# Two mixture-of-experts layers on one core: expert rows stored by halves and blended in place, first loads and the tile table moved ahead of the borders

## The chip, the cores and the metric

The kernel runs on one core of a Trainium2 chip. The metric is the device time of one launch in microseconds (us); the median of 3 runs before the change is 739.51 us (737.39 to 741.89). The engines are TensorE (PE, with its weight loads as PEld), VectorE (DVE), ScalarE (ACT), GpSimd (POOL) and SyncE (SP). SP and ACT issue plain DMAs, POOL issues indirect ones (scatters whose destination rows come from an index tile).

## The reference

32 sequences of 128 tokens with 128 channels (4096 tokens) pass through two layers.

- Layer 0: each sequence is scaled by a style vector made from its condition, projected, normalised by a factor, biased and clipped. Then a feed-forward stage: every token chooses the 2 best of 8 experts (`top_k` of `x @ Wg`), their weights are a softmax of the two logits, each expert computes `silu(x W1) * (x W2) @ W3` with 176 hidden channels, and a shared expert of 352 hidden channels is added.
- Layer 1: an adapter conditioned on the sequence (128 to 32 to 128, ReLU, residual); then layernorm, attention with 16 heads of 8 channels and a residual; then layernorm, again the 2 best of 8 experts, each `relu(h W1 + b1) @ W2 + b2` with 512 hidden channels, weighted and added to the stream. The output is `(32, 128, 128)` float32.

What matters for the change: each token ends as `x + w_a * expert_a(h) + w_b * expert_b(h)`, a sum of its stream row and two expert rows.

## The kernel before

`build` runs six blocks one after another: `layer0`, `experts0`, `pre_attention`, `attention`, `experts1`, `finish`. Each block gives every engine its own instruction list; a block ends with a barrier of all engines. SBUF holds the stream `m.X` (partition = token in the sequence, 32 sequences of 128 channels), and the arrays `m.V` (attention's values) and `m.X3` (the stream after the adapter) of the same shape.

**Routing.** Tokens go in 8 groups of 4 sequences. `choose_*` (DVE) finds the two best experts, `route_rank` (PE) counts places within an expert, `index_*` (DVE) gives each (token, choice) a row of the DRAM buffer `dispatch_rows`, and POOL scatters the rows there (`route_scatter`, L341, 8 indirect DMAs of 128 rows per group). Each row carries 128 channels, its destination row in `expert_rows` (slot `SLOT_ID`, copied from `m.ids` at L310) and its softmax weight. The destination row of (sequence s, token p, choice k) is `2 * (128 s + p) + k`, so the two rows of a token lie side by side; the choice is 0 for the better expert.

**The tile table.** Each expert's rows are cut into tiles of 256; there are always 39 tiles (`ETILES`), the most that can be needed, and those past the last real one hold padding rows. After the last group, `table_vector` (DVE, L397 to L420) computes for every tile its expert and its first row; its first instruction (L397) writes where each expert's rows end and raises `ended`, its last ones raise `tabled`. On `ended`, SP fills the rest of the last tile of experts 0 to 3 with padding (`table_fill`, L371) and ACT that of experts 4 to 7. SP then waits for all fills to land (`tails`); POOL waits for all scatters. Then comes the barrier.

**Experts.** In `experts0` and `experts1` SP reads for every tile two entries of the table (`value_load`) and issues two DMAs: 256 rows (`xs` at L859, `xt` at L1841, 130 KB) and the expert's weights (`w` at L861, 304 KB; `wb` at L1843, 578 KB). There are 8 load buffers (`EB`). PE turns the rows (L766), multiplies in three float32r products (L816) and projects down (L893, L1872); ACT and DVE split and evacuate; POOL scatters two times 128 rows per tile to `expert_rows` (L825). PE's order at the start is: turn tile 0, turn tile 1, up-products of tile 0, then for each n: turn n + 2, up n + 1, down n. In `experts1` the last step on a tile is DVE's `leave` (L1883), which adds the bias, and POOL's scatter follows.

**Finish.** SP fetches the two rows of each token in 8 groups of 512 KB (`fetch_rows`, L948) into 4 buffers, DVE adds the first row to `m.X` (L978) and the second to that (L981), and ACT stores each group of 256 KB (L987).

In `attention` DVE's list carries, beside the softmax work of sequence s, the routing of earlier groups cut into pieces between the maxima (L1570): `choose_hot` (L280, L281), `index_place` (L305 to L314).

## Time and profile before

| what | value |
|---|---|
| profiled execution, its own time | 738.1 us |
| its span, first to last instruction | 736.3 us |
| median of 3 runs | 739.51 us |
| PE busy, share of span | 588.9 us, 80% |
| DVE busy | 490.2 us, 67% |
| POOL busy | 448.7 us, 61% |
| ACT busy | 370.1 us, 50% |
| mean granted TensorE clock | 0.903 |

The span is from the first to the last instruction of the profiled execution; its own time is 1.8 us longer and takes in what lies around it. The engines' busy times are sums over stages with different limits, so no one of them is the time: the page's slices show PE at 9 tenths or more in the two expert stages and in attention, and well below that in the slices (18 us each) before either expert stage is under way and at the end.

### The profile page before, as it was taken

To read this page: it belongs to the slowest core of one execution; us is meant where nothing else is said; L and a number is where in the kernel's file an instruction comes from. 1 tells how busy PE (TensorE), PEld (TensorE's weight loads), DVE (VectorE), ACT (ScalarE), POOL (GpSimd) and SP (SyncE) were. 2 spreads that over 40 slices of the span, in tenths; PEclk is the share of its full clock that TensorE was granted. 3 is DMA by queue.
4 is the path that set the end of the run, shared out by engine and by line. 5 is a ranking of instruction groups with operands and counts; after the bars stand their busy time and mean duration, and the time that the engine had idled before them with its cause. 6 is when DMAs were issued, how large, how long until landed. Compare 5 with 4: busy or idle time off the path is not lost. (4 is left out here: it accounts for less than half of the span.)

```text
span 736.3 us, 17755 instructions
## 1 busy us (share of the span) xinstructions
PE 588.9 (80%) x5538; PEld 473.9 (64%) x5538; DVE 490.2 (67%) x1502; ACT 370.1 (50%) x798; POOL 448.7 (61%) x588
## 2 busy tenths in 40 slices
PE   4999935999992787737999999999920999999940
PEld 2566625989892555415766766676620999999940
DVE  3566434767671689755878878877652678878735
ACT  3444303655561344335777777777520556556520
POOL 2677741766677658274455887797763256666640
PEclk9999976999996599967999999999955899999985
DMA  7911146767773267715553444444117988888429
GB/s 223 244 57 52 55 94 163 213 198 207 201 212 103 71 187 220 222 68 104 102 119 85 132 108 132 105 125 123 44 40 162 314 258 246 260 242 248 138 66 314
DMA packets 97978, 115.24 MB, mean 157 GB/s; under 512 B 16144, under 2 KB 77616, under 8 KB 97776
## 3 DMA queue, kind: packets, MB, share of 16 engines
q1 hardware_dynamic: 82368, 92.36, 46.8%
q0 software_dynamic: 9088, 18.76, 7.8%
q10 hardware_dynamic: 6448, 3.20, 1.8%
q8 instruction: 38, 0.62, 0.4%
q14 instruction: 36, 0.29, 0.2%
HBM read 80.75 MB, written 33.53 MB: 155 GB/s over the span
## 5 line engine op out<-in xcount | busy, mean ns | idle before, releaser
L341 POOL DMA_INDIRECT dispatch_rows<-row,index x128 | 126.0, 984 | 56.9 <-issue 33.7
L825 POOL DMA_INDIRECT expert_rows<-fo,to x78 | 84.0, 1076 | 68.2 <-DVE fo L1883 54.8
L1570 DVE TENSOR_REDUCE mneg<-ps 128x4 f32<-128x512 f32 x128 | 86.6, 679 | 43.4 <-PE ps L1711 42.6
L825 POOL DMA_INDIRECT expert_rows<-eo,to x78 | 74.7, 958 | 52.6 <-ACT eo L918 30.2
L1661 ACT ACTIVATE prob<-ps 128x512 f32<-128x512 f32 x128 | 75.4, 589 | 54.2 <-PE ps L1723 53.5
L798 DVE CAST xh<-psT 128x256 fp32r<-128x256 f32 x78 | 33.1, 424 | 73.8 <-PE psT L766 73.6
L1872 PE MATMUL psO<-wb,fh 128*128 128x128 f32 x624 | 75.9, 275 | 0.0
L1711 PE MATMUL ps<-km,qp 96*128 96x512 f32 x128 | 63.2, 500 | 14.0 <-POOL km L1508 12.7
L1654 ACT ACTIVATE km<-kp,const 96x512 fp32r<-96x512 f32 x96 | 67.7, 712 | 11.0 <-PEq L1045 5.5
L816 PE MATMUL psA<-xh,wh 128*128 128x256 f32 (+1 forms) x234 | 73.1, 312 | 0.0
L1872 PEld LDWEIGHTS psO<-wb,fh 128*128 128x128 f32 x624 | 73.1, 192 | 0.0
L816 PE MATMUL psA<-xh,wl 128*128 128x256 f32 (+1 forms) x234 | 66.7, 285 | 0.0
L816 PE MATMUL psA<-xl,wh 128*128 128x256 f32 (+1 forms) x234 | 66.6, 285 | 0.0
L1508 POOL TENSOR_SCALAR km<-kp,const 96x512 fp32r<-96x512 f32 x32 | 54.4, 1701 | 14.4 <-POOLq L1045 13.0
L1721 PE MATMUL ps<-qm,kp 96*128 96x512 f32 x128 | 52.3, 409 | 3.0 <-DMA qm<-qk_parts 2.9
L1723 PE MATMUL ps<-mxT,selr 128*128 128x512 f32 x128 | 51.4, 402 | 0.0
L1918 ACT ACTIVATE fw<-psO,xt 128x128 f32<-128x128 f32 x78 | 24.4, 364 | 44.1 <-PE psO L1872 28.8
L1711 PEld LDWEIGHTS ps<-km,qp 96*128 96x128 f32 x128 | 25.5, 200 | 28.4 <-issue 21.4
L790 ACT ACTIVATE wh<-w 128x352 fp32r<-128x352 f32 x39 | 19.4, 497 | 47.3 <-DMA w<-in_W 44.8
L816 PEld LDWEIGHTS psA<-xl,wh 128*128 128x128 f32 (+1 forms) x234 | 42.7, 183 | 0.0
L816 PEld LDWEIGHTS psA<-xh,wh 128*128 128x128 f32 (+1 forms) x234 | 42.7, 182 | 0.0
L816 PEld LDWEIGHTS psA<-xh,wl 128*128 128x128 f32 (+1 forms) x234 | 42.5, 182 | 0.0
(193 smaller groups left out, 1505.2 us busy)
## 6 DMA issues: line engine op xcount, KB each, us to landing
wb<-in_W1b SPq DMA_DIRECT2D x39, 578.0 KB
w<-in_W SPq DMA_DIRECT2D x39, 304.0 KB
qk_parts<-qk SPq DMA_DIRECT2D x8, 1024.0 KB, 5.0
qp<-qk_parts SPq DMA_DIRECT2D x48, 128.0 KB, 2.8
kp<-qk_parts SPq DMA_DIRECT2D x48, 128.0 KB, 3.4
qm<-qk_parts SPq DMA_DIRECT2D x192, 32.0 KB
xs<-dispatch_rows SPq DMA_DIRECT2D x39, 130.0 KB
xt<-dispatch_rows SPq DMA_DIRECT2D x39, 130.0 KB
```

The lines of the kernel that those rows point to most:

```text
L341: pool.indirect_dma_start(out=m.xbuf, out_offset=bass.IndirectOffsetOnAxis(ap=r.index[b][:, c:c + 1], axis=0), in_=r.row[b][:, c // TOPK, ...
L798: v.tensor_copy(z.xh[q][:], z.psT[:, q, 0:SLOTS]).then_inc(z.x_high, 1)
L816: ins = z.m.nc.tensor.matmul(out, w[k][q][:, columns], x[k][q][:], start=(k == 0), stop=(k == 2), skip_group_check=True)
L825: pool.indirect_dma_start(out=m.ybuf, out_offset=bass.IndirectOffsetOnAxis(ap=to[b][:, a:a + 1], axis=0), in_=out[b][:, a, :], in_offset=N ...
L1508: ins = nc.gpsimd.tensor_scalar(km[s % 2][:, :, j, :], kp[side(s)][:, :, tok(s)].bitcast(F32), mask(j), None, ALU.mult)
L1570: nc.vector.tensor_reduce(mneg[s % 2][:, g, :], ps1[:, g % 2, :].rearrange("p (j k) -> p j k", j=4), AX_X, ALU.max, negate=True).then_inc( ...
L1654: nc.scalar.activation(km[s % 2][:, :, j, :], kp[side(s)][:, :, tok(s)].bitcast(F32), ACT.Copy, scale=mask(j)).then_inc(km_act, 1)
L1661: nc.scalar.activation(prob[s % 2][:, g, :], ps2[:, g % 2, :], ACT.Exp, scale=ATT_SCALE).then_inc(exped, 1)
L1711: nc.tensor.matmul(ps1[:, g % 2, :], qp[side(s)][:, g, tok(s)], km[s % 2][:, g].rearrange("p j k -> p (j k)"), start=True, stop=True).then ...
L1721: nc.tensor.matmul(ps2[:, g % 2, :].rearrange("p (j k) -> p j k", j=4), kp[side(s)][:, g, tok(s)], qm[(s // 2) % 2][:, g, :, tok(s)], star ...
L1723: nc.tensor.matmul(ps2[:, g % 2, :], selr[:, g, :], mxT[s % 2][:].rearrange("p j k -> p (j k)"), start=False, stop=True).then_inc(shifted, 1)
L1872: ins = nc.tensor.matmul(psO[:, q, a * P:(a + 1) * P], h[q][:, k, a * P:(a + 1) * P], wb[b][:, WIDE + k * P:WIDE + (k + 1) * P], start=(k ...
```

## The change

1. Router 1 (`halves=True`) writes another destination row: `32 p + s`, plus 4096 (`TOK`) if the choice's expert has the higher number of the two. So `expert_rows` holds a lower half (the rows of each token's lower expert) and an upper half, and a partition's 32 rows of a half are contiguous (16 KB). It costs one more comparison in `choose_hot` and two `scalar_tensor_tensor` in place of one copy in `index_place`.
2. The table gets 8 more entries: for each of the 4 output buffers, how many sends are done once the tiles of experts 0 to 6 (lower half complete) and once all real tiles (upper half complete) are scattered (`table_sends`, layer 1 only).
3. At the end of `experts1` SP waits for those counts, fetches the lower half into `m.V` in 4 DMAs of 512 KB, waits for the second counts and fetches the upper half into `m.X3`. DVE, after its last `leave`, adds both in place into `m.X`; ACT stores. The block `finish` and its barrier are gone.
4. All eight padding fills are issued by SP; ACT's part is gone.
5. After the fills, still in `layer0` and in `attention`, SP loads tiles 0 and 1 of the coming expert stage (`lead_loads`): the weights once the table stands, the rows once all fills and scatters have landed. The expert stage's own loop on SP starts with tile 2. In layer 1 the loads land in an arena shared with attention's `prob`.
6. In `layer0` the table is computed in pieces inside the loop over groups 6 and 7, not after it.

The renamed semaphores of `layer0` (`formed`, `pe_set`) count the same events as the ones they replace. The constant tile grows by 64 columns.

```diff
 def index_place(r, dve, n, rank):
...
-    nc.vector.tensor_copy(r.row[side][:, :, :, SLOT_ID:SLOT_ID + 1].bitcast(U32),
-                          m.ids[:, n * GT:(n + 1) * GT, :].unsqueeze(3))
+    if r.halves:
+        rows = m.const[:, C_ROW:C_ROW + SEQS * TOPK].rearrange("p (s k) -> p s k", k=TOPK)
+        for k, half in ((0, float(TOK)), (1, -float(TOK))):
+            nc.vector.scalar_tensor_tensor(out=r.row[side][:, :, k, SLOT_ID].bitcast(U32), in0=r.later[b][:], scalar=half,
+                                           in1=rows[:, n * GT:(n + 1) * GT, k], op0=ALU.mult, op1=ALU.add)
...
 def table_sync(w, sp):
...
-    table_fill(w, sp, range(E // 2))
-    sp.wait_ge(w.tails, 16 * (E + 1))
+    table_fill(w, sp, range(E))
...
+def table_sends(w, dve):
...
+    c(v.memset(w.real[:], 0.0))
+    for a in range(2):
+        ins = v.tensor_tensor(w.real[:, a, 0:ETILES], tl, bc(w.incl[:, E - 2 + a:E - 1 + a], P, ETILES), ALU.is_lt)
+    c(ins)
+    c(v.tensor_reduce(w.sends[:], w.real[:].rearrange("p a (i q) -> p a q i", q=OB), AX_X, ALU.add))
+    c(v.tensor_scalar(m.table[:, DONE:DONE + 2 * OB], w.sends[:].rearrange("p a q -> p (a q)"), 32.0, None, ALU.mult))
...
@@ layer0, DVE's loop over groups
+                    if n == GROUPS - 1:
+                        table_rows(tiles, dve)
                     gate(n, 2)
+                    if n == GROUPS - 1:
+                        table_end(tiles, dve)
                     if n + 3 < GROUPS:
                         scale(n + 3)
+                    if n == GROUPS - 2:
+                        table_counts(tiles, dve)
                     if n + 1 < GROUPS:
                         gate(n + 1, 0)
+                    if n == GROUPS - 2:
+                        table_experts(tiles, dve)
...
+def lead_loads(m, sp, tiles, scattered, weights, w, xs):
+
+    sp.wait_ge(tiles.tabled, 1)
+    rows = []
+    for b in range(LEAD):
+        e = sp.value_load(m.table[0:1, b:b + 1], min_val=0, max_val=E - 1)
+        sp.dma_start(w[b], weights[bass.ds(e, 1)].rearrange("e p h -> (e p) h")).then_inc(m.ld[b], 16)
+        rows.append(sp.value_load(m.table[0:1, b + ETILES:b + ETILES + 1], min_val=0,
+                                  max_val=E * REGION + (E - 1) * SLOTS))
+    sp.wait_ge(tiles.tails, 16 * (E + 1))
+    for sem, total in scattered:
+        sp.wait_ge(sem, total)
+    for b in range(LEAD):
+        sp.dma_start(xs[b], m.xbuf[bass.ds(rows[b], SLOTS), :].rearrange("(a p) c -> p a c", p=P)).then_inc(m.ld[b], 16)
...
@@ experts1, SP (after its loop over the tiles)
+                for a, to in enumerate((m.V, m.X3)):
+                    for b in range(OB):
+                        sends = sp.value_load(m.table[0:1, DONE + OB * a + b:DONE + OB * a + b + 1], min_val=0, max_val=32 * 10)
+                        sp.wait_ge(st[b], sends + 32 * uses(b, OB))
+                        sp.sem_inc(m.passed, 1)
+                    mine = m.ybuf[a * TOK:(a + 1) * TOK, :].rearrange("(p s) c -> p s c", s=SEQS)
+                    for h in range(HALVES):
+                        part = slice(h * HS1, (h + 1) * HS1)
+                        sp.dma_start(to[:, part, :], mine[:, part, :]).then_inc(upper[h] if a else lower, 16)
...
@@ experts1, DVE (after its last leave)
+                def blend(n, a):
+                    h, mine, rows, sem = n * GT // HS1, slice(n * GT, (n + 1) * GT), (m.V, m.X3)[a], m.blends[a]
+                    dve.wait_ge(upper[h] if a else lower, (0 if a and h else came_before) + (16 if a else 16 * HALVES))
+                    if a:
+                        dve.wait_ge(m.blends[0], GROUPS + n + 1)
+                    nc.vector.tensor_tensor(m.X[:, mine, :], rows[:, mine, :], m.X[:, mine, :], ALU.add).then_inc(sem, 1)
+
+                blend(0, 0)
+                for n in range(GROUPS):
+                    if n + 1 < GROUPS:
+                        blend(n + 1, 0)
+                    blend(n, 1)
...
@@ experts1, ACT (after its last weigh)
+                for n in range(GROUPS):
+                    act.wait_ge(m.blends[1], GROUPS + n + 1)
+                    act.dma_start(out_rows[n * GT:(n + 1) * GT].rearrange("s p c -> p s c"), m.X[:, n * GT:(n + 1) * GT, :]
+                                  ).then_inc(m.stored, 16)
+                act.wait_ge(m.stored, 16 * GROUPS)
```

## Rows read from the trace of the kernel before

**Rows 1.** Busy time by stage: us; PE, PEld, DVE, ACT, POOL; PEclk; DMA share; GB/s.
```profile
150.00:170.00 20.00, 18.39 (x151) 17.28 (x150) 13.27 (x35) 10.85 (x27) 12.81 (x15) 1.00 0.71 200
586.00:680.00 94.00, 94.00 (x823) 94.00 (x823) 75.09 (x218) 55.41 (x138) 59.72 (x56) 1.00 0.86 253
680.00:700.00 20.00, 20.00 (x177) 20.00 (x177) 15.93 (x48) 11.88 (x30) 13.00 (x13) 1.00 0.46 139
```

**Rows 2.** Timeline of SP's queue before experts0 (start us, length us, instruction, count).
```profile
101.64 4.10 SPq L371 DMA_DIRECT2D dispatch_rows<-tail  x4
...
112.47 0.42 SPq L859 DMA_DIRECT2D xs<-dispatch_rows  x1
...
118.09 0.35 SPq L861 DMA_DIRECT2D w<-in_W  x1
```

**Rows 3.** Timeline of ACT's queue and of POOL at the same place.
```profile
101.56 4.29 ACTq L371 DMA_DIRECT2D dispatch_rows<-tail  x4
...
102.64 0.96 POOL L341 DMA_INDIRECT dispatch_rows<-row,index  x1 [0.31 <-issue]
```

**Rows 4.** Timeline of PE, the start of experts0: the second tile turned.
```profile
118.96 0.69 PE L766 MATMUL psT<-const,xs 128*128 128x128 f32 x2 [1.97 <-DMA w<-in_W]
```

**Rows 5.** Timeline of DVE at the end of layer0.
```profile
94.41 0.69 DVE L545 TENSOR_TENSOR h<-psB,s 128x512 f32<-128x512 f32 x1 [4.16 <-PE psB L676]
...
100.46 0.17 DVE L397 CAST table<-base 128x8 int32<-128x8 f32 x1
```

**Rows 6.** Timeline of SP's queue and of ACT, late in experts0.
```profile
205.60 0.35 SPq L861 DMA_DIRECT2D w<-in_W  x1
...
208.87 0.50 ACT L790 ACTIVATE wh<-w 128x352 fp32r<-128x352 f32 x1 [0.41 <-DMA w<-in_W]
```

**Rows 7.** Timeline before experts1: SP's queue, POOL's last scatter, PE's second and third tile.
```profile
551.19 4.28 SPq L371 DMA_DIRECT2D dispatch_rows<-tail  x4
564.43 0.39 SPq L1841 DMA_DIRECT2D xt<-dispatch_rows  x1
...
569.48 0.34 SPq L1843 DMA_DIRECT2D wb<-in_W1b  x1
...
559.55 0.96 POOL L341 DMA_INDIRECT dispatch_rows<-row,index  x1 [0.30 <-issue]
...
572.22 0.69 PE L766 MATMUL psT<-const,xt 128*128 128x128 f32 x2 [2.70 <-DMA wb<-in_W1b]
...
575.27 0.63 PE L766 MATMUL psT<-const,xt 128*128 128x128 f32 x2
```

**Rows 8.** Timeline of DVE in attention, one lap that routes a group.
```profile
443.92 0.14 DVE L280 TENSOR_TENSOR diff<-best 128x4 f32<-128x4 f32 x1
443.99 0.21 DVE L281 TENSOR_TENSOR hot<-choice,const 128x64 f32<-128x64 uint32 x1
...
454.07 0.69 DVE L1570 TENSOR_REDUCE mneg<-ps 128x4 f32<-128x512 f32 x1 [1.24 <-PE ps L1711]
```

**Rows 9.** Timeline of the end: experts1's last scatters and the finishing block.
```profile
703.23 0.95 POOL L825 DMA_INDIRECT expert_rows<-fo,to  x1 [0.31 <-issue]
...
708.69 0.61 DVE L1883 SCALAR_TENSOR_TENSOR fo<-wb,xt,fw 128x128 f32<-128x128 f32 x2 [1.17 <-ACT fw L1918]
...
711.70 0.96 POOL L825 DMA_INDIRECT expert_rows<-fo,to  x1 [0.30 <-issue]
714.45 10.70 SPq L948 DMA_DIRECT2D fr<-expert_rows  x8
718.86 0.69 DVE L978 TENSOR_TENSOR fp<-fr,X 128x512 f32<-128x512 f32 x1 [9.55 <-DMA fr<-expert_rows]
...
732.68 0.69 DVE L981 TENSOR_TENSOR fo<-fr,fp 128x512 f32<-128x512 f32 x1
```

**Rows 10.** DMA: the whole core while the rows are fetched; POOL's queue in 600 to 680.
```profile
717.00:718.00 1.00, 0.00 (x0) 0.00 (x0) 0.00 (x0) 0.00 (x0) 0.00 (x0) 0.50 1.09 384
...
q0 software_dynamic: 1468, 3.01, 10.0%
```

More of the change, by code:

```diff
@@ L200, with __init__ @@
 class Router:
-    def __init__(self, m, ctx, tag, bias, deep):
-        self.m, self.bias, self.deep = m, bias, deep
+    def __init__(self, m, ctx, tag, bias, deep, halves=False):
+        self.m, self.bias, self.deep, self.halves = m, bias, deep, halves
+        if halves:
+            self.later = [m.sb(f"later{tag}{b}", [P, GT], ctx=ctx) for b in range(2)]
         self.logits = [m.sb(f"logits{tag}{b}", [P, GT, E], ctx=ctx) for b in range(2)]
@@ L495, in _ @@
                 table_sync(tiles, sp)
+                lead_loads(m, sp, tiles,
+                           [(r.scattered[b], r.sends * len(range(b, GROUPS, ROW_BUFFERS))) for b in range(ROW_BUFFERS)],
+                           d["W123"], [w[:] for w in m.lead_w], [x[:] for x in m.lead_xs])
             @block.gpsimd
@@ L731, in _ @@
                     lower(n)
-EB = 8
-OB = EB // 2
 def uses(b, of):
@@ L1039, in pre_attention @@
         m.blends = blend1, blended
-        came = m.sems("p_came0", "p_came1")
+        m.stored = m.sem("stored")
+        m.rows_in = m.sems(*(f"rows_in{b}" for b in range(1 + HALVES)))
+        came = m.rows_in[0:2]
         gbu_in = m.sems("p_gbu0", "p_gbu1")
@@ L1431, in post_scatter, with late_buffers @@
     route_scatter(q.router, pool, n, b, q.rows_done, part)
+LATE_W = 2 * KT1 * P + KT1 + P
+def late_buffers(m, ctx):
+    m.arena = m.sb("arena", [P, 2 * HG * 4 * P], F32, ctx)
+    area = m.arena
+    m.late_w = [area[:, b * LATE_W:(b + 1) * LATE_W] for b in range(LEAD)]
+    at = LEAD * LATE_W
+    m.late_xs = [area[:, at + b * 2 * ROW:at + (b + 1) * 2 * ROW].rearrange("p (a c) -> p a c", a=2) for b in range(LEAD)]
 def attention_loads(m, ctx):
@@ L1455, in attention @@
         mxT = two("mxT", [P, 4, P], F32R)
-        prob = two("prob", [P, HG, 4 * P])
+        prob = [m.arena[:, b * HG * 4 * P:(b + 1) * HG * 4 * P].rearrange("p (g k) -> p g k", g=HG) for b in range(2)]
         rec = two("rec", [P, P])
@@ L1499, in _ @@
                 table_sync(tiles, sp)
+                sp.wait_ge(mixed, SEQS)
+                lead_loads(m, sp, tiles, [(sem, post.router.sends * GROUPS // 2) for sem in post.router.scattered],
+                           d["W1b"], m.late_w, m.late_xs)
             @block.gpsimd
@@ L1942, in build @@
         allocate(m, d)
-        layer0(m, d)
-        experts0(m, d)
-        with ExitStack() as middle:
-            attention_loads(m, middle)
-            pre_attention(m, d)
-            attention(m, d)
-        experts1(m, d)
-        finish(m, d, out)
+        with ExitStack() as front:
+            lead_buffers(m, front)
+            layer0(m, d)
+            experts0(m, d)
+        with ExitStack() as back:
+            late_buffers(m, back)
+            with ExitStack() as middle:
+                attention_loads(m, middle)
+                pre_attention(m, d)
+                attention(m, d)
+            experts1(m, d, out)
 def laid_out(a):
```

138 lines of the change are left out of this document (69 added, 69 removed).

## Prediction

> **What bounds the kernel now.** I read the page's slices first: PE is near full except in three places, the borders before the two expert stages and the end. Then the stages' busy times, then the timelines of SP's queue, POOL, DVE and PE at each of the three places. What the reader is to see:
>
> - In experts1 PE is busy the whole time at full clock (94.00 of 94.00 us) and DMA has 14% to spare [rows 1]. In experts0 PE has gaps (18.39 of 20.00 us), and ACT waits for weights whose DMA SP issued only 3 us earlier [rows 1, 6]: tile loads come at the pace of SP's loop. So an expert stage ends as much earlier as its stream of loads, or its first tiles, start earlier.
> - First border: PE starts the second tile at 118.96 [rows 4], though POOL's last scatter was issued by 103.60 [rows 3]. Between stand the padding fills, issued by two queues from 101.6 to 105.9 [rows 2, 3], their landing, the barrier, and SP's first loads from 112.47.
> - Second border: the last scatter ends at 560.51, the first load is issued at 564.43, PE turns the second tile at 572.22 and the third, without a wait, at 575.27 [rows 7].
> - End: DVE's last `leave` ends at 709.30, the last scatter at 712.66, the fetch starts at 714.45, the first blend at 718.86, the last ends at 733.37, the span at 736.3 [rows 9]. DMA runs at 384 GB/s in between [rows 10]; 4 MB in and 2 MB out bound the block.
>
> Two constants I use below. From the end of the last scatter to the first DMA of the next block without table reads: 714.45 − 712.66 = 1.79 us [rows 9]; I split it into 1.3 for the landing and 0.5 for the barrier (the split is a choice, the sum is measured). With two table reads ahead it is 564.43 − 560.51 = 3.92 [rows 7], so the reads and the entry cost 2.13.
>
> **Part 1, first border.** The table moves into DVE's gaps (4.16 us idle before 94.41 [rows 5]). `ended` then comes after the gate that ends where this idle time begins, 94.41 − 4.16 = 90.25, where it came at 100.46. The DVE work added before the last gates (about 3 us over two groups) delays the shared expert by at most that, and that ends by 100.5, 3 us before the last scatter: cost nothing. If that cover were gone it would be 3 us. POOL scatters back to back at 1.26 us (0.96 + 0.30 [rows 3]) and is moved by nothing. SP's fills: (4.28 − 0.42) / 3 = 1.29 us each [rows 7] (0.42 is one issue [rows 2]), so eight take 7 × 1.29 + 0.42 = 9.5, from 91.3 to 100.8. Behind them stand four table reads (0.87 each at most: a fill's 1.29 less its 0.42 issue) and two weight issues, 3.9 us: to about 104.7. The scatters' landing is 103.60 + 1.3 = 104.9, so the two chains tie. The row loads are issued at about 105.0 and 105.6, ending at 106.1. Barrier 0.5 and entry 2.13: tile 2's rows at 108.7, its weights 0.6 later at 109.3, where they were at 118.09 [rows 2]: 8.8 earlier. Tile 1 stands at about 105.6 + 3 = 108.6, where PE had it at 118.96: 10 earlier. Since SP's stream paces the stage, I take the smaller: **8.9**. Bounds: 6.5 (SP's chain 2.4 late, as if nothing of the table's move came early enough) to 10.4.
>
> **Part 2, second border.** Here the table cannot move, `ended` stays at 550.3, and SP now issues eight fills where it and ACT issued four each: last fill ends at 551.19 + 9.45 = 560.6. The table end comes some 1.1 us later for the six small instructions of `table_sends`, at about 556, hidden under the fills. Four table reads (0.75 in the middle) and two weight issues: 564.4; that is later than the scatters' landing (561.8), so SP is the late one now. Row loads to 565.5, barrier and entry 2.6: tile 2's rows at 568.1, its weights at 568.7 against 569.48 [rows 7], only 0.8 earlier. Tile 1 is complete at about 568 against 572.22 (4 earlier), but then PE needs tile 2 after 2.75 us of up-products. A tile's weights take 3.8 to 4.9 us from issue to use here (the third tile's, issued 569.48, were there by 575.27 without a wait [rows 7]), so tile 2 is ready at 572.5 to 573.6 against 575.27. I take **2.2**; bounds 0 (the four fills more and the reads eat it all) to 4.2 (tile 1 decides).
>
> **Part 3, attention.** DVE works without a gap in two laps of four, then waits 1.24 us for PE [rows 8]; PE is full, so a delay in the gapless laps carries on. Added per group: one comparison and one more small instruction, each at the pitch of the small ones, 0.07 us (443.92 to 443.99 [rows 8]), up to 0.14 busy. 6 groups inside the laps × 0.15 = **−0.9**. Bounds 0 (the wait takes it up) to −2.4 (8 × 0.3). The last group's index is 0.3 us ahead of POOL and costs nothing.
>
> **Part 4, the end.** From the reference's inputs I counted the tokens of layer 1's experts: 36 of 39 tiles are real, 24 of them of experts 0 to 6. Tile 35's second scatter ends at 704.18 [rows 9], landed 705.5. The lower half is fetched from about 686 on, when SP has issued its last tile; DMA then has over half to spare (share 0.46 [rows 1]). The upper half: issue 705.7, 4.4 us to the first landing as in the old block (714.45 to 718.86 [rows 9]) gives 710.1, then each 512 KB in 1.4 us at 384 GB/s [rows 10]: 711.5, 712.9, 714.3. DVE's first blend starts behind the last `leave`, 709.35. The 16 blends: an add of this shape takes 0.69, a pitch between 0.61 (waits already met) and 0.72; I take 0.65, so the last ends at 709.35 + 15 × 0.65 + 0.69 = 719.8. Each piece of the upper half is there before its blend. The stores follow at one per 1.3 us; the last takes the old 736.3 − 733.37 = 2.93. End 722.7, against 736.3: **13.6**. Bounds 12.4 (pitch 0.72) to 14.2 (0.61), and 6 if the fetch turns out late (rival 2). Work removed: one barrier, the block entry, the wait for the three padding tiles' scatters, and the 4 MB fetch from behind the last tile. What is late next is DVE's own 10.4 us.
>
> The remaining edits (renamed semaphores; 32 KB more constants, loaded beside 0.5 MB; the arena, the same size as `prob`) cost nothing.
>
> **Sum.** 8.9 + 2.2 − 0.9 + 13.6 = 23.8. Against the profiled execution's own 738.1 us: 714.3. That execution lies 1.4 under the median of 739.51; I forecast between the two scales, **715 us**. Its own range, from the bounds above, is 710 to 721.
>
> **A rule against the change.** The row of the fetch shows 384 GB/s for reads in 1 KB pieces that lie one behind the other [rows 10]. The change reads 4 KB pieces 16 KB apart, and scatters neighbouring tokens 16 KB apart where they were 1 KB. The Trainium skill, page "DMA: Bandwidth & Descriptors", section "Latency and other measured facts", states that a per-partition row pitch in HBM at large powers of two slows copies: 207 GB/s at 512 KiB, 103 at 4 MiB. It gives no figure for 16 KiB, and no run here shows one. By its 207 GB/s the upper half would be complete at about 718.8, still just ahead of its last blends, and the sum would stay; by 103 it would lose some 9 us. What it would do is rival 2.
>
> **Rivals.**
>
> 1. *SP, now alone with the fills and reads, is late at both borders.* For it: SP's queue is the later one at the second border by 2.6 us by my own working, and ties at the first. Against: at the first there is no work on SP before `ended`. It gives 3 to 4 less at the first border and 2.2 less at the second: 715 + 6 = 721. Chance 0.15.
> 2. *The 16 KB pitch halves or quarters the fetch.* For it: nothing in the profile has this pitch. Against: bytes per piece grow fourfold. At a quarter of 384 GB/s (5.5 us per piece) the last piece lands at 705.7 + 4.4 + 4.1 + 3 × 5.5 = 730.7 and the end is 735: 715 + 12 = 727. Chance 0.06.
> 3. *Slower than before: the scatter's pitch.* POOL's queue takes 10.0% of the 16 engines in experts1 and 14% are spare [rows 1, 10]. If a scattered row cost 2.4 times its time, DMA would bind; it becomes a loss from the point where the stage's 134 us grow by 24, a share of 1.18, or 4.2 times per row. At 5 times: 0.86 + 0.40 = 1.26, 35 us more: 750. Against: rows of an expert's tile are already far from adjacent. Chance 0.02.
> 4. *More than forecast:* tile 1 decides at both borders and the blends run at 0.61: 10.4 + 4.2 + 14.2 = 28.8, 709.5. Chance 0.1.
> 5. *It does not start the fetch early*, because the counts hold SP until nearly all scatters are done. The end then is 714 + 4.4 + 10.4 + 2.9 = 731.7: 4.6 instead of 13.6, 724. Chance 0.05.
>
> Forecast itself: 0.62. The range that leaves out no more than 2 in 10: **708 to 723**. This kernel's runs tell no change from one of about 0.5% (3.7 us). Faster by more than that: all cases but rival 3 and remnants, 0.96; within: 0.02; slower: 0.02.
>
> **What would show it.** Part 1: SP's first tile-loop load near 108.7, PE's second tile turned near 108.8, the stage's scatters ending near 222 instead of 230.9. Part 2: eight fills in about 9.5 us; the interval from POOL's last dispatch scatter to PE's third tile 12.5 where it was 14.8. Part 3: the distance from attention's first score to its last longer by about 1. Part 4: lower fetch right behind SP's last tile load, upper fetch about 1.5 us behind tile 35's second scatter; sixteen adds without a wait for DMA; 13.4 us from the last `leave` to the end where it was 27.0. It is wrong if blends wait for the upper half, if PE waits for weights through experts1, or if the first border gives under 6.5.

## The result: 720.6 us where 715 was forecast

The changed kernel takes 720.64 us (median of 4 runs, 719.23 to 721.5). The kernel before took 740.7 in the same comparison (737.39 to 744.48). The ratio is 0.973, 95% interval 0.967 to 0.978: 2.7% faster, 20 us. The profiled execution takes 720.71 with a span of 718.3; before it was 738.1 and 736.3. By the spans the gain is 18.0 us, where my sum had 23.8.

The end and the second border gave about what was worked out. The first border gave a little less. A stage that I had not mentioned, `pre_attention`, took back 4.9 us, though its code is the same. Intervals below are in us, from the start of the span, and a stage's length is the distance between two events of the two profiles.

The page of the changed kernel, parts 1 to 3, to be held against the page shown of the kernel before:

```profile
span 718.3 us, 17794 instructions
...
PE 590.8 (82%) x5538; PEld 475.2 (66%) x5538; DVE 495.0 (69%) x1523; ACT 369.9 (51%) x798; POOL 445.6 (62%) x588
...
PE   4999959999991876637999999999961499999992
...
PEclk9999997999996599966999999999985599999997
DMA  7921156677763255734434344343413988888858
```

In the last two slices PE stood at 4 and 0 tenths before; now at 9 and 2.

**First border.** SP's queue (start, length):

```profile
90.72 8.92 SPq L389 DMA_DIRECT2D dispatch_rows<-tail  x8
100.43 2.07 SPq L814 DMA_DIRECT2D lead_w<-in_W  x2
106.51 0.95 SPq L821 DMA_DIRECT2D lead_xs<-dispatch_rows  x2
109.19 0.37 SPq L930 DMA_DIRECT2D xs<-dispatch_rows  x1
109.75 0.34 SPq L932 DMA_DIRECT2D w<-in_W  x1
```

The fills start at 90.72 where they stood at 101.64 [rows 2]. The third tile's weights are issued at 109.75, 8.34 us earlier than there. POOL's last scatter ends at 103.87, where it was 103.60 [rows 3]. Whether the table inside DVE's gaps delayed layer 0 can't be told from that: three more profiles of the same layer have 102.63 to 103.78 (e1, e2, e4 below). The lead rows leave 2.64 us after that end; SP waited 3.1 us there, for these scatters to land. The last scatter of experts0 ends 7.57 us earlier (223.31 against 230.88).

**pre_attention.** From the end of that scatter to the start of POOL's last addition in the stage (L1113) it takes 77.02 us, before 72.09. One group in the middle, DVE and POOL, of the changed kernel:

```profile
257.70 1.27 POOL L1113 TENSOR_TENSOR X<-x,rows 128x512 f32 x1
...
259.59 2.30 DVE L1315 TENSOR_SCALAR norm<-x,mv,rstd 128x128 f32<-128x128 f32 x4 [0.16 <-DVE rstd L1312]
260.14 0.46 POOL L1121 TENSOR_TENSOR wdt<-dproj,gbD 128x128 f32<-128x128 f32 x1 [1.18 <-DMA gbu<-cond_rows]
260.56 1.25 POOL L1122 TENSOR_TENSOR wut<-uproj,gbu 32x512 f32<-32x512 f32 x1
...
266.34 0.61 POOL L1112 COPY X<-x 128x512 f32 x1 [2.66 <-DVE x L1176]
```

and of the kernel before:

```profile
265.00 1.26 POOL L1082 TENSOR_TENSOR X<-x,rows 128x512 f32 x1
...
266.89 1.29 DVE L1284 TENSOR_SCALAR norm<-x,mv,rstd 128x128 f32<-128x128 f32 x4 [0.16 <-DVE rstd L1281]
267.64 0.46 POOL L1090 TENSOR_TENSOR wdt<-dproj,gbD 128x128 f32<-128x128 f32 x1 [1.39 <-DMA gbu<-cond_rows]
268.06 1.27 POOL L1091 TENSOR_TENSOR wut<-uproj,gbu 32x512 f32<-32x512 f32 x1
...
272.35 0.61 POOL L1081 COPY X<-x 128x512 f32 x1 [0.26 <-DVE x L1145]
```

Before, POOL's first product `wdt` begins 0.75 us after DVE's norm, and the norm takes 1.29. After, it begins 0.55 after it, the norm takes 2.30, and POOL's COPY of the next lap waits 2.66 us where it waited 0.26. From one COPY to the next there are seven laps. The first two (7.55 and 9.59) and the last (6.5) are the same in both kernels. The four in the middle take 8.86 to 9.21 us, in the kernel before 7.76 to 7.92. Of a long lap's 1.2 us the norm has 1.0 and DVE's `part`, the first addition of the blend, 0.2 to 0.4 (it takes 0.84 to 1.09 where it took 0.67). The norm's median instruction is as fast as ever, but single ones stand still until POOL's product ends: in the lap shown the fourth starts at 260.60, `wut` ends at 261.81, and the norm at 261.89. By line (min/median/max ns), the changed kernel, then the kernel before, whose first two norms are long as well:

```profile
L1315 DVE TENSOR_SCALAR norm<-x,mv,rstd x32: 334/347/1301, 242.4 to 302.9; 128x128 f32<-128x128 f32 x32
L1284 DVE TENSOR_SCALAR norm<-x,mv,rstd x32: 334/344/1298, 249.8 to 305.5; 128x128 f32<-128x128 f32 x32
```

**Attention** takes what it took: from POOL's last addition of pre_attention to its last dispatch scatter's end 257.20, before 257.54. DVE is busy for 1.3 us more in it (185.8 against 184.5).

**Second border.** SP's queue, then ACT and PE:

```profile
548.16 8.48 SPq L389 DMA_DIRECT2D dispatch_rows<-tail  x8
556.57 0.96 POOL L358 DMA_INDIRECT dispatch_rows<-row,index  x1 [0.30 <-issue]
557.53 2.16 SPq L814 DMA_DIRECT2D arena<-in_W1b  x2
560.90 0.96 SPq L821 DMA_DIRECT2D arena<-dispatch_rows  x2
563.57 0.37 SPq L1898 DMA_DIRECT2D xt<-dispatch_rows  x1
...
565.26 1.15 ACT L859 ACTIVATE wh<-arena 128x512 fp32r<-128x512 f32 x2 [20.20 <-DMA arena<-dispatch_rows]
...
570.15 0.63 PE L835 MATMUL psT<-const,xt 128*128 128x128 f32 x2
...
574.65 0.38 PE L835 MATMUL psT<-const,xt 128*128 128x128 f32 x2
```

The third tile is turned at 570.15, without a wait, 12.62 us after POOL's last scatter; before it was 14.76 [rows 7]. From the fourth tile on the stage has its steady pace of 3.43 us. The fourth is turned 17.12 after that scatter, before 18.66 (579.17 after 560.51): 1.5 us are left.

**experts1.** From the fourth tile turned to the last `leave` 130.83 us, before 130.13. The one new wait stands beside the fetch of the lower half (four pieces from 683.90 on, landing after 5.0 to 8.1 us):

```profile
689.65 0.61 DVE L1949 SCALAR_TENSOR_TENSOR fo<-arena,fw 128x128 f32<-128x128 f32 x2
...
692.64 0.17 DVE L878 COPY to<-xt 128x2 uint32<-128x2 uint32 x1 [2.39 <-DMA expert_rows<-fo,to]
...
694.78 0.61 DVE L1949 SCALAR_TENSOR_TENSOR fo<-wb,xt,fw 128x128 f32<-128x128 f32 x2
...
697.42 0.61 DVE L1949 SCALAR_TENSOR_TENSOR fo<-wb,xt,fw 128x128 f32<-128x128 f32 x2
```

The distance of two leaves is 5.13 there instead of 3.43, and then 2.64.

**The end.** DVE's blends, by line:

```profile
L1976 DVE TENSOR_TENSOR X<-V,X x8: 679/682/686, 705.4 to 713.3; 128x512 f32<-128x512 f32 x8
L1976 DVE TENSOR_TENSOR X<-X x8: 679/683/737, 706.6 to 714.5; 128x512 f32<-128x512 f32 x8
```

The first begins where the last `leave` ends (705.48), none waits for a DMA, and the mean pitch is 0.61 (15 steps from 705.40 to 714.54). The last ends at 715.23, the span at 718.3. The window of 705 to 710 shows 402 GB/s, above the 384 of the old block [rows 10]; the first stores, from 707.37 on, are in it. From the last `leave` to the end 12.8 us, before 27.0 [rows 9].

Summed: 7.6 (first border, with layer 0) − 4.9 (pre_attention) + 0.3 (attention) + 1.5 (second border) − 0.7 (experts1) + 14.2 (end) = 18.0.

### The profile page after: what moved, and what is told of

It reads as the page before. It is cut to its first block, busy times and chain, and to the rows that moved or that the text cites. A ratio compares the mean times of both kernels' runs of the same rounds, so it can differ in the third digit from the quotient of the medians.

```text
span 718.3 us, 17794 instructions
## 1 busy us (share of the span) xinstructions
PE 590.8 (82%) x5538; PEld 475.2 (66%) x5538; DVE 495.0 (69%) x1523; ACT 369.9 (51%) x798; POOL 445.6 (62%) x588
## 4 chain that ended last, share of the span: by engine, by line
PE 29%; POOL 13%; issue 8%; DVE 3%; DMA 2%; SPq 0%; ACT 0%; DVEq 0%; POOLq 0%
PE psO L1938 10%; PE psA L885 8%; POOL dispatch_rows L358 7%; PE ps L1761 2%; PE ps L1771 2%; PE psAO L1791 2%; PE psAO L1800 2%; PE ps L1773 2%; POOL vb L1575 1%; POOL km L1555 1%; PE psT L835 1%; POOL X L1384 1%; POOL rstd L1377 1%; DVE X L1976 1%; DMA arena<-dispatch_rows 1%
## 5 line engine op out<-in xcount | busy, mean ns | idle before, releaser
L894 POOL DMA_INDIRECT expert_rows<-fo,to x78 | 84.0, 1078 | 67.3 <-DVE fo L1949 53.8
L1712 ACT ACTIVATE arena<-ps 128x512 f32<-128x512 f32 x128 | 75.4, 589 | 53.4 <-PE ps L1773 52.5
L894 POOL DMA_INDIRECT expert_rows<-eo,to x78 | 74.7, 958 | 44.7 <-issue 23.1
L1555 POOL TENSOR_SCALAR km<-kp,const 96x512 fp32r<-96x512 f32 x32 | 54.4, 1701 | 13.5 <-POOLq L1076 12.8
L1938 PE MATMUL psO<-wb,fh 128*128 128x128 f32 x464 | 56.5, 275 | 0.5 <-ACT fh L2008 0.5
L1938 PEld LDWEIGHTS psO<-wb,fh 128*128 128x128 f32 x464 | 54.3, 192 | 0.7 <-ACT fh L2008 0.7
L1997 ACT ACTIVATE fw<-psO,xt 128x128 f32<-128x128 f32 x58 | 18.1, 364 | 33.6 <-PE psO L1938 27.0
L1791 PE MATMUL psAO<-arena,vb 128*32 128x128 f32 x1024 | 34.6, 276 | 0.0
```

The lines of the kernel that those rows point to most:

```text
L894: pool.indirect_dma_start(out=m.ybuf, out_offset=bass.IndirectOffsetOnAxis(ap=to[b][:, a:a + 1], axis=0), in_=out[b][:, a, :], in_offset=N ...
L1555: ins = nc.gpsimd.tensor_scalar(km[s % 2][:, :, j, :], kp[side(s)][:, :, tok(s)].bitcast(F32), mask(j), None, ALU.mult)
L1712: nc.scalar.activation(prob[s % 2][:, g, :], ps2[:, g % 2, :], ACT.Exp, scale=ATT_SCALE).then_inc(exped, 1)
L1791: nc.tensor.matmul(psO[32 * g:32 * g + 32, p, 0:P], vb[p][:, 4 * g + j, :], prob[p][:, g, j * P:(j + 1) * P], start=(j == 0), stop=(j == 3 ...
L1938: ins = nc.tensor.matmul(psO[:, q, a * P:(a + 1) * P], h[q][:, k, a * P:(a + 1) * P], wb[b][:, WIDE + k * P:WIDE + (k + 1) * P], start=(k ...
```

## The experiments

Twelve runs of ten kernels, in three comparisons: e1 and e9 are the changed kernel again, and e6 and e12 are one kernel. They ran on three chips, and these are not alike. On the first (e1 to e4) the kernel before takes 737.4 us, close to what it takes above; on the second (e5 to e8) 817.8 and on the third (e9 to e12) 810.9. So times are compared within one comparison alone, and intervals are read from the traces, one profile of each run. The second comparison has no run of the changed kernel and no profile of the kernel before. e8, which differs from the changed kernel at the end alone, stands in for it at the borders.

**The loop in pre_attention.** e1 is the changed kernel once more.

> The changed kernel once more, as the measure for the other three. The profile of it that I have loses 4.9 us in pre_attention, whose code the change doesn't touch: a group takes 9.1 us there where it took 7.9 in the kernel before, and the normalising TENSOR_SCALAR of DVE takes 629 ns in the mean instead of 380. Theory A (a loop with two stable timings): the norm overlaps POOL's modulation products by a little more or less, and which timing it falls into hangs on a few tenths of a us at the stage's start; the kernel can then come out with 9.1 or with 7.9, its time 720.6 or about 716. Theory B (the change itself slows the stage, by where its tiles now lie): always 9.1, time 719.5 to 721.5. A and B are told apart better by the next two kernels.

Measured: 719.83 (717.63 to 724.03), ratio to before 0.9745 (0.969 to 0.9799). Its four middle laps take 7.88, 9.13, 8.97 and 9.06 us: they start with the short timing and change to the long one. The stage takes 76.00. The long timing is not there from the start, so the tiles' places alone don't make it.

e2 adds one wait:

```
 if not late(n):
+    pool.wait_ge(normed, n + 1)
     modulate(n + 2, b, i + 1)
```

> The changed kernel, with one wait more in pre_attention: POOL computes the modulation of group n+2 only when DVE has normalised group n. Theory A (the norm is slow because POOL's products run beside it): norm falls to 320 to 340 ns per instruction in every group, the group's period to 7.9 us or less, the kernel becomes 4 to 5 us faster than the changed one: about 716. Theory B (placement of the tiles): norm stays near 630 ns and the period at 9.1; time 720 to 722, since POOL only starts later. A third way: the products now fall beside the blend's additions and slow those instead; period between, 718.

Measured: 716.32 (714.17 to 718.72), 3.5 less than e1 beside it. By the two ratios to the kernel before (0.9713 and 0.9745) it is 2.4, and their intervals (0.9659 to 0.9767 and 0.969 to 0.9799) overlap, so the traces must carry this:

```profile
264.94 1.12 DVE L1316 TENSOR_SCALAR norm<-x,mv,rstd 128x128 f32<-128x128 f32 x4 [0.16 <-DVE rstd L1313]
...
266.25 0.46 POOL L1121 TENSOR_TENSOR wdt<-dproj,gbD 128x128 f32<-128x128 f32 x1 [1.94 <-DVE norm L1316]
266.67 1.26 POOL L1122 TENSOR_TENSOR wut<-uproj,gbu 32x512 f32<-32x512 f32 x1
267.30 1.19 DVE L1150 TENSOR_TENSOR part<-gr,X 128x512 f32<-128x512 f32 x1
```

The norm's mean is 343 ns over all 32 instructions (583 in the changed kernel), so theory A holds for it. But `part` now runs beside POOL's `wut` and takes 1.19 us instead of 0.67, so the middle laps take 8.2 to 8.4, not 7.9: the third way that I had named. The stage takes 71.13 us, 5.9 less than in the changed kernel. Of that the four middle laps give 2.9. The second lap falls from 9.59 to 7.39, for its norm was long in the kernel before too, the first grows by 0.3, and 1.1 lie ahead of the first lap.

e3 is the same wait in the kernel before.

> The kernel before, with the same wait added in pre_attention. Theory A (two timings): the kernel before ran from 737.4 to 744.5 in its single runs, because it falls into either; with the wait it should always have the short one: all runs within 1.5 us of each other, at 736 to 738, while the runs of the kernel before beside it are spread over 4 to 7 us. Theory B (the kernel before always has the short timing): nothing gained, the same spread as the kernel before, 738 to 744.

Measured: 739.27 (736.52 to 740.1, 10 runs) beside 737.4 (735.09 to 742.46, 13 runs); ratio 1.0014, 0.9986 to 1.0041. The spread shrinks from 7.4 to 3.6 us where I expected 1.5, and nothing is gained in the median: the middle laps are 8.1 to 8.4 and not 7.9, and the stage takes 73.2 us where it took 72.1. Whether the middle laps of the kernel before also change to the long timing in some runs stays open: the one profile of it unchanged shows none.

Over all profiles without the wait the stage's length follows the count of long laps among the four middle ones, whichever chip it is: 0 of them 72.1 us (before); 2 of them 75.0 (e4), 75.0 (e6), 74.7 (e7); 3 of them 76.0 (e1), 75.9 (e5), 75.9 (e11), 76.1 (e12); 4 of them 77.0 (after), 77.5 (e8), 77.2 (e9). One distance sorts these 44 laps without an exception, the start of `wdt` less the start of the norm: it is 0.60 us or more in all 14 short laps and 0.58 or less in all 30 long ones. In e6 and e7 the fourth of them is short again, so neither timing, once entered, lasts for certain.

**The fetch beside the last tiles.** e4 spreads the four pieces of the lower half:

```
 for h in range(HALVES):
     part = slice(h * HS1, (h + 1) * HS1)
+    if a == 0:
+        sp.wait_ge(evac, ETILES - 7 + h)
     sp.dma_start(to[:, part, :], mine[:, part, :])...
```

> The changed kernel, with the four 512 KB pieces of the lower half fetched one per tile of experts1 (piece h waits for the 32+h-th leave) where they were issued together at 683.9. Theory: the 2 MB fetched at 332 to 338 GB/s held up the completion of POOL's scatters, so that DVE's COPY of the places waited 2.39 us for them at 692.6, and PE with it. Paced, that wait goes, from the second border's third tile turned to the last leave it takes about 1.3 to 2.4 us less: 718.5 to 719.5, last leave near 703.5 instead of 705.48. Rival: the wait comes from something else of the last tiles (loads of the last tiles, 4 KB rows): it stays at 2 us or more and the time at 720.6.

Measured: 718.43 (717.53 to 720.7), 1.4 less than e1 in the median, but with the same ratio to the kernel before (0.9743 and 0.9745), and its profile has one long lap less: the total shows nothing. The pieces leave from 682.26 to 692.1 and land after 4.0 to 4.6 us, and DVE's COPY of the places waits for no DMA in experts1 any more (2.9 us in all in the changed kernel, 2.8 in e1, 3.8 in e2; 0.8 in the kernel before).

```profile
688.01 0.60 DVE L1951 SCALAR_TENSOR_TENSOR fo<-arena,fw 128x128 f32<-128x128 f32 x2
688.53 0.16 DVE L878 COPY to<-xt 128x2 uint32<-128x2 uint32 x1
...
691.44 0.60 DVE L1951 SCALAR_TENSOR_TENSOR fo<-wb,xt,fw 128x128 f32<-128x128 f32 x2
691.96 0.16 DVE L878 COPY to<-xt 128x2 uint32<-128x2 uint32 x1
```

From the fourth tile turned to the last `leave` it takes 130.09 us, as in the kernel before (130.13); unpaced it is 130.83, 130.79 (e1) and 130.88 (e2). So the cause is shown, and its price is 0.7, not the 1.3 to 2.4 that I expected: after the stall the leaves come 2.64 and 2.43 apart, and DVE catches up with PE. (The rate in the expectation, 332 to 338 GB/s, is that of single windows of 1 us; from 684 to 694 the mean is 267.)

**The end.** e5 keeps the borders and goes back to the old end (interleaved rows, finishing block, no fetch in experts1):

```
-self.router = Router(m, ctx, "1", ..., 2, halves=True)
+self.router = Router(m, ctx, "1", ..., 2)
-            experts1(m, d, out)
+            experts1(m, d, out)
+            finish(m, d, out)
```

> The changed kernel with the old end: layer 1's rows interleaved by token again, no fetch and no blend in experts1, the finishing block after it; the table's move and the lead loads stay. Theory (the gains are separate: 7.6 at the first border, 1.5 at the second, 14.2 at the end): last leave to the end of the span 27.0 us, as in the kernel before; DVE's COPY of the places no longer waits for DMA in experts1, and from the fourth tile turned to the last leave it takes 130.1 instead of 130.8; total 720 + 14.2 - 0.7 = 733.5, within 731 to 736 because pre_attention can take 72 to 77 us. Rival (16 KB pitch of the scatters cost the stage something that the end pays back): experts1 becomes faster than 130.1.

Measured: 810.27 beside 817.8 for the kernel before: ratio 0.991 (0.9875 to 0.9942). The changed kernel has 0.979 (0.9754 to 0.9833) on the third chip, a slow one too. From the last `leave` (783.26) to the end of the span (809.3) 26.0 us; in every kernel with the new end except e8 (below) it is 12.75 to 12.9, on all three chips. So the end is worth 13 to 14 us, alone. The expected total was for the first chip. On the rival this run says nothing: experts1 takes 139.9 us from the fourth tile on, within the 138.9 to 143.0 of the kernels with the new end and the unpaced fetch on these chips. The first chip answers it: with the scatters at the 16 KB pitch and the fetch paced, e4 takes 130.09, with the old scatters the kernel before takes 130.13.

e8 lets the lower half wait for the same counts as the upper.

```
-sends = sp.value_load(m.table[0:1, DONE + OB * a + b:...])
+sends = sp.value_load(m.table[0:1, DONE + OB + b:...])
```

> The changed kernel, but the lower half's fetch waits for the same counts as the upper's, so that all 4 MB are fetched behind the last real tile. Theory: the first fetch is issued at about 701 and lands 4 us later; 4 MB at 400 GB/s take 10.5 us, the last piece is there at 716 to 717 where its blend began at 714.5; the first blends wait; the last leave comes 0.7 earlier, since nothing is fetched beside the last tiles. From last leave to end 12.8 becomes 15.5 to 17; net 2 to 3.5 us slower: 722.5 to 724. Rival (fetch rate is no limit at the end, DVE's blends are): less than 1 us slower.

Measured: 803.34; last `leave` at 783.60, span 799.7: 16.1 us from one to the other, 3.3 more than 12.8. The range expected (15.5 to 17) holds it, and its rival falls. DVE's blends now wait twice:

```profile
786.05 1.29 DVE L1976 TENSOR_TENSOR X<-V,X 128x512 f32<-128x512 f32 x2 [2.45 <-DMA V<-expert_rows]
788.03 0.69 DVE L1976 TENSOR_TENSOR X<-X 128x512 f32<-128x512 f32 x1 [0.69 <-DMA X<-expert_rows]
```

So the early fetch of the lower half gives 3.3 at the end, less the 0.7 that it costs beside the last tiles. The expected total was for the first chip.

**The borders.** e7 computes layer 0's table behind the last addition again.

```
-if n == GROUPS - 2:
-    table_counts(tiles, dve)
...
 add(GROUPS - 1)
+table_counts(tiles, dve)
+table_experts(tiles, dve)
+table_rows(tiles, dve)
+table_end(tiles, dve)
```

> The changed kernel with layer 0's table computed behind the last addition again (as before the change), the rest as changed: SP alone then makes eight fills from 101.5 on. Theory (the move of the table is what the first border's gain rests on): fills 101.5 to 110.5, lead rows at 114 to 115, rows of tile 2 at 117 to 118 against 109.2; the stage ends 8 us later, so the lead loads alone give about nothing here. Time 728. Rival: the lead loads carry half of it: 4 us later only, 724.

Measured: 808.02 beside 803.34 (e8) and 802.86 (e6). Its SP queue:

```profile
128.01 8.82 SPq L389 DMA_DIRECT2D dispatch_rows<-tail  x8
137.62 2.07 SPq L810 DMA_DIRECT2D lead_w<-in_W  x2
140.58 0.95 SPq L817 DMA_DIRECT2D lead_xs<-dispatch_rows  x2
143.27 0.37 SPq L926 DMA_DIRECT2D xs<-dispatch_rows  x1
```

From POOL's last scatter in layer 0 to the last scatter of experts0 165.7 us, against 156.7 in e8 on the same chip: 9.0. That is as much as the whole gain of the first border and more (119.44 against 127.28 for the same distance on the first chip, 7.8). So the move of the table carries this gain. The two chips differ here, though: the late fills start 5.9 us after the last scatter (122.07), and in the kernel before on the first chip they start 2 us before its end. That lead loads alone give nothing is likely and not shown: e7 also has all eight fills on SP. The totals of this comparison agree with it: e7 is 9.8 us faster than the kernel before, and the new end alone is worth 13 to 14.

e6 has the table's move and no lead loads (the loop over two tiles runs zero times, and experts0 and experts1 load from tile 0 on).

> The changed kernel without the two tiles loaded ahead at either border; the table's move and the end stay. Theory: at the first border the loads of the third tile come behind four loads of the first two, each pair 2.2 us apart: rows of tile 2 are issued 12 to 13 us after POOL's last scatter begins to land, where they were 5.3 after its end; PE's third tile 3 to 4 later, stage end 3 later. At the second border the same, 1.5 to 3 later. Time 724.5 to 727. Rival: SP's landing waits are the limit, not the loads: less than 1 us lost at each border.

Measured: 802.86, beside 803.34 for e8, which is 2.6 slower at the end by the above. Third tile of experts0 turned 16.4 us after the last scatter, in e8 15.7: the rival's "less than 1 us", not the 3 to 4 of the theory. Fourth tile of experts1 22.3 after the last scatter, in e8 19.4 and in e5 20.3. e12 is the same kernel on the third chip.

> The changed kernel without lead loads, once more; on the other chip they were worth 0.7 us at the first border (last scatter to third tile turned 16.4 instead of 15.7) and 2.0 to 2.9 at the second (fourth tile turned 22.3 after the last scatter instead of 19.4 to 20.3). Theory 1: on a chip whose POOL ends layer 0 at 103.9, SP has the lead weights out before the scatters land, so the lead is worth more here: 2 to 3 us at the first border, 2.5 at the second; 725. Rival: 0 to 1 and 2.5: 723.

Measured: 799.51, beside 796.41 for the changed kernel (e9). Third tile of experts0 20.2 against 15.8 in e9; fourth of experts1 20.5 against 19.9. So the first tiles of a stage come 0.6 and 4.4 earlier by the lead at the first border and 0.6 to 2.9 at the second. What is left of it when the stage ends is another matter. From the last scatter before experts0 to its last scatter e6 takes 156.3 against 156.7 in e8, e12 157.9 against 155.5 in e9. From the last scatter before experts1 to its last `leave` e6 takes 162.9 against 159.9, e12 159.4 against 161.0. The sign changes from pair to pair, so what the lead is worth stays open. On these chips SP finishes the fills at 124.9 to 127.4, after the last scatter (121.1 to 123.0), so neither pair says what it is worth where SP is ready first.

e11 puts the weights behind the rows:

```
 for b in range(LEAD):
     sp.dma_start(xs[b], ...).then_inc(m.ld[b], 16)
+    sp.dma_start(w[b], ...).then_inc(m.ld[b], 16)
```

> The changed kernel; at both borders the lead tiles' weights go out behind their rows, so that nothing of SP's is in the queues while the last scatters land. Theory (608 KB of weights in the queues stretch the landing from 1.3 to 2.6 us at the first border): rows are issued 1.3 us behind the end of the last scatter instead of 2.64; the weights then arrive 4 us later, so tile 0 is turned no earlier, and the stage ends 0 to 2 us later: 720 to 723. Rival (the landing takes 2.6 by itself, the split 1.3 + 0.5 in my forecast was wrong): rows 2.5 to 2.8 behind the last scatter here too.

Measured: 798.97 (2 runs). It doesn't answer its question: SP's fills end at 126.08, 4.8 us after POOL's last scatter, so SP never waits for the landing. Why the lead rows leave 2.35 to 3.1 us after the last scatter's end on the first chip (four profiles) and not 1.3 stays open. At the second border it answers another question: with one row load of 130 KB ahead in place of a tile's weights, a lead tile's weights still take 4.4 us from issue (628.14) to first use (632.50).

**The three edits together.** e9 is the changed kernel as the measure, e10 has e2's wait, e4's pacing, and four of the second border's eight fills issued by ACT.

```
-table_sync(tiles, sp)
+table_sync(tiles, sp, range(E // 2))
...
+table_fill(tiles, act, range(E // 2, E))
```

> The changed kernel once more, as the measure on the chip of this comparison: on a chip where the kernel before takes 735 to 742 us, 718 to 722; on one where it takes 810 to 825, about 800. In the profile pre_attention's laps take 7.9 us up to some lap and 9.1 from there on, as in three profiles so far.

> The changed kernel with three edits: the norm's wait in pre_attention, the lower fetch paced by the leaves, and the padding fills of the second border shared by SP and ACT again (four each). Theory: the first is worth 3.5 us (716.3 against 719.8 measured), the second 0.7 (last leave to fourth tile turned 130.1 instead of 130.8), the third 1.5 to 2 (eight fills end at 552 instead of 556.6, the lead weights go out 4 us earlier, the lead rows only at the scatters' landing, 1.3 us behind the last scatter instead of 3.4, and are not behind 1.16 MB of weights: from the last scatter to the fourth tile turned 15.3 instead of 17.1). Sum 5.5 to 6 below the changed kernel: 714 where that takes 720. Rival for the third: the lead rows' landing takes 4.4 us because of the queue itself, not of the weights ahead: then 16.3 to 17.

Measured: e9 796.41 (790.99 to 801.87), ratio to before 0.979 (0.9754 to 0.9833). e10 787.95 (786.9 to 791.6), ratio 0.9715 (0.968 to 0.975). In e9's profile all four middle laps of pre_attention are long, where I expected a short start. The intervals of the ratios just don't meet. The medians are 8.5 us apart, the ratios 6.3, so the 5.5 to 6 expected is not refuted. The two profiled executions are 11.7 apart (e9's is its slowest). Of that pre_attention has 4.6 (72.6 against 77.2), the second border 1.9 (fourth tile 18.0 against 19.9 after the last scatter), experts1 3.0 (138.1 against 141.1). Layer 0 has 1.9 and experts0 1.2, which none of the three edits touches, and attention takes 0.7 back: that is how far two executions lie apart on this chip. How much of the 3.0 is the pacing can't be said: without it this stage varies from 138.9 to 143.0 on the slow chips, and on the first the pacing gave 0.7. In e10 SP and ACT at the second border:

```profile
609.88 5.03 ACTq L389 DMA_DIRECT2D dispatch_rows<-tail  x4
609.89 8.58 SPq L389 DMA_DIRECT2D dispatch_rows<-tail  x4
620.63 2.04 SPq L814 DMA_DIRECT2D arena<-in_W1b  x2
623.49 0.95 SPq L821 DMA_DIRECT2D arena<-dispatch_rows  x2
627.21 1.15 ACT L859 ACTIVATE wh<-arena 128x512 fp32r<-128x512 f32 x2 [20.72 <-DMA arena<-dispatch_rows]
```

Tile 0 is there 8.3 us after the last scatter (618.96), 10.8 in e9. Both sub-steps that I expected fail, though: SP's four fills alone take 8.58 here, so the rows leave 4.5 us behind the scatter and not 1.3.

## Why the prediction was right in sign and 5.6 us off

**End: mechanism and size held.** Forecast 13.6, measured 14.2. The pitch came to 0.61 where I took 0.65 (bounds 0.61 to 0.72), and the upper half, whose fetch left at 701.91, was there before its blends. The last `leave` to the end took 12.8 instead of 13.4. The lower half was not hidden for free, as I had it ("DMA then has over half to spare"): it cost 0.7 in experts1. My share was that of the tile loads alone; with the fetch beside them DMA stood at 0.79 from 684 to 694, and the completion of POOL's scatters came late. e4 shows the cost and e8 what the early fetch gives for it, 3.3.

**First border: 8.9 forecast, 7.6 measured**, inside the bounds of 6.5 to 10.4. (By its own figures, 118.09 less 109.3, the forecast should have read 8.8.) The fills took 8.92 from 90.72 (forecast 9.5 from 91.3), so SP was ready early and waited 3.1 us. The mis-sized term is the landing of the scatters: 1.3 taken, 2.64 measured, so the lead rows were issued 1.6 late. Barrier and entry gave 0.9 of that back: from the last lead row's issue to the third tile's rows it takes 1.73 where I had 2.63. The split of the 1.79 into 1.3 and 0.5 was a choice, as I said there, and a wrong one. The third tile's rows came at 109.19 instead of 108.7. The rest is that experts0 did not keep all it was given: the weights came 8.34 earlier and the stage ended 7.57 earlier. It is also one profile: from layer 0's last scatter to the end of experts0 the changed kernel gains 7.8 here, and 6.2 to 7.6 in e1, e2 and e4.

**Second border: 2.2 forecast; 2.1 at the third tile, 1.5 at the fourth.** Here the size was right by luck. I had said that tile 2 decides, waited for by PE, at 572.5 to 573.6. It did not: PE turned it without a wait at 570.15. The rows of the two lead tiles decided. Those of tile 0 were there 4.4 us after their issue (560.90 to 565.26), with 1.16 MB of lead weights issued ahead of them. That those weights are the reason is not shown. In e10 the rows take 3.7 with the same weights ahead, and in e11 a tile's weights take 4.4 with almost nothing ahead. SP was late by my working, 2.6 behind the landing. It was not: its fills ended at 556.64, and SP then waited 0.4 us for the last scatter to land, which took 3.4 and not 1.3. In e4 it waited 0.3, in e1 and e2 not at all, so the two chains tie.

**Attention: −0.9 forecast, +0.3 measured.** The stage's length goes with the clock that TensorE was granted in it, a mean over its two levels: 257.2 to 257.8 us at 0.90 of full speed (three profiles with the change; 257.54 in the kernel before at the same 0.90), 258.9 at 0.89 (e3, without the change) and 260.6 at 0.88 (e1). At one clock no 0.9 is lost, though DVE is busy 1.3 us longer. So my step, that a delay in DVE's gapless laps carries on because PE is full, failed. That DVE's wait for PE (1.24 us in each lap of four) took the small instructions up is the likely reason and was the lower bound that I had named.

**What was missing: pre_attention, −4.9.** It is the step that failed. I counted every instruction that the change moves, and took a stage whose instructions don't change as unchanged. Its laps have two timings, and the sum had no line for it. In the profile before, the laps of 7.9 us, with POOL's `wut` starting 0.12 us before the end of DVE's norm, were the sign, and the second lap of 9.59, whose norm is long, even more so. With 0.2 us of shift one of four norm instructions stands still until `wut` ends (1301 ns where the median is 347; `wut` takes 1.25 us). Then the norm ends a us later, SP issues the next `gbu` 1.8 us behind that end (as in the kernel before), it lands 5.2 later, and `wdt` of the next lap falls beside the next norm again. e2 shows that the overlap is the cause, since the stage loses the long norms with it. Ten profiles of kernels with the change and without the wait show 2 to 4 long laps, the one of the kernel before none. That the change favours the long timing is likely by that count, but one profile is little; why it would is open. That the total stayed inside the range is luck in this part: the range was made for other risks.

The rule of the Trainium skill for this stands in "SBUF — State Buffer", section "Who interferes with whom": `tensor_scalar` is among the operations that can enter a mode that takes the port pair shared with GpSimd, a DVE instruction with two SBUF inputs contends with a GpSimd instruction that reads SBUF, and the one that comes second is blocked until the other ends. The trace agrees in both: the norm, a `tensor_scalar`, with its 1301 ns, and in e2 the two-input `part` with 1.19 instead of 0.67.

**Rivals.** The 16 KB pitch slowed nothing: 402 GB/s in the fetch, and a scatter of experts1 takes POOL 1078 ns in the mean, before 1076. The rule of the Trainium skill on large row pitches ("DMA: Bandwidth & Descriptors", section "Latency and other measured facts"), whose figures begin at 512 KiB, does not reach down to 16 KiB here. The counts did start the fetch early, right behind the last tile load. SP, alone with the fills, was late at neither border in this profile.

**Against my signs.** Third tile's rows 109.19 (108.7 forecast), second tile turned 109.49 (108.8), experts0's scatters end 223.3 (222), third tile of experts1 12.6 after the last scatter (12.5), upper fetch 1.4 behind its scatter (1.5): these held to 1.3 us or better. Attention by 1 longer: wrong.

## What to carry to other kernels

An edit elsewhere in a kernel may change the timing of a loop shared by two engines. Before summing, look in each later loop for an instruction pair that ends and starts within some tenths of a us, and give it a term in the range. A bulk fetch put beside a tuned stage should be cut into pieces and paced by that stage's own counter: what suffered here was the completion of small transfers that others wait for. And a stall of 2.4 us in a row isn't a loss of 2.4: measure from a point before it to the next point where the bounding engine is the limit again.

## What I had not expected of the hardware

Three chips gave 737, 818 and 811 us for the same kernel before, and the change was worth 2.7% on the first and 2.1% on the third. In the changed kernel on the third chip layer 0 ends 19 us later (122.97 against 103.87), experts0 takes 36 more (155.5 against 119.4), attention 13 and experts1 10; pre_attention takes the same 77 and the end the same 12.8. In experts1 the first 22 tiles keep their 3.43 us on it, and from tile 23 on every two tiles take 8.4 instead of 6.9. There both DVE and ACT stand still at once, for a releaser called `remote`:

```profile
723.60 0.87 DVE L1962 TENSOR_SCALAR fh<-psA,arena 128x256 f32<-128x256 f32 x2
...
726.60 0.63 ACT L1997 ACTIVATE fw<-psO,xt 128x128 f32<-128x128 f32 x2 [2.73 <-remote]
727.26 0.42 DVE L867 CAST xh<-psT 128x256 fp32r<-128x256 f32 x1 [2.79 <-remote]
```

What the engines wait for there isn't told by the profile, and no run here tests it. None of the six profiles from before, after and e1 to e4 has this releaser, and each of the eight on the two other chips has it more than 50 times. For this study it means that a total from one chip is no measure on another. Intervals between two events of one stage can still be compared where that stage is free of such waits, as pre_attention and the end are.
